# Two mixtures of experts: outputs stored and gathered, or scaled by GpSimd and added by indirect DMA into two sums

## What is computed

```python
expert_weight, expert_idx = jax.lax.top_k(probs, TOP_K)
expert_weight = expert_weight / jnp.sum(expert_weight, axis=-1, keepdims=True)
...
inter = jnp.square(jax.nn.relu(inter))
outb = jnp.einsum('ecf,edf->ecd', inter, w2_stack)
flat_out = outb[sorted_e, local_pos] * sorted_w[:, None]
moe_out = jnp.zeros((t, Cc), x.dtype).at[sorted_tok].add(flat_out)
```

## Time and profile before

| | |
|---|---|
| median of 3 runs | 1416.88 us (1414.7 to 1422.69) |
| the profiled execution | 1425.25 us |
| its span, first to last instruction | 1423.4 us |
| mean granted clock of TensorE | 0.878 of full |
| TensorE busy | 1079.6 us, 76% |
| VectorE busy | 748.6 us, 53% |
| ScalarE, GpSimd busy | 385.5 us and 357.9 us |
| moved by DMA | 113.59 MB |

### The profile page before, as it was taken

One profiled execution on the slowest core, in us unless ns is written; L12 is line 12 of the kernel. 1 busy time (PEld: TensorE's weight loads), 2 busy tenths in 40 slices (PEclk: granted clock), 3 DMA queues, 4 the chain that ended last, 5 costly groups with the idle time before them and its releaser, 6 DMA issues.

```text
span 1423.4 us, 16288 instructions
## 1 busy us (share of the span) xinstructions
PE 1079.6 (76%) x5482; PEld 882.7 (62%) x5482; DVE 748.6 (53%) x1778; ACT 385.5 (27%) x705; POOL 357.9 (25%) x290
## 2 busy tenths in 40 slices
PE   1987989788746673788999747989897159999940
PEld 0646766477545653566878535868685058999840
DVE  5467555565533436355556553454535536666642
ACT  1204022031123324224242232332422023333310
POOL 4204144040402234411010131010101432224235
PEclk9999989999878996799999957989999569999985
DMA  8700014000156652100000010000000664636435
GB/s 265 238 1 30 0 63 130 1 0 0 60 176 194 177 182 69 43 17 0 1 0 0 15 58 16 1 1 0 0 1 1 195 189 141 185 109 217 148 97 169
DMA packets 91887, 113.59 MB, mean 80 GB/s; under 512 B 6577, under 2 KB 77489, under 8 KB 91697
## 3 DMA queue, kind: packets, MB, share of 16 engines
q1 hardware_dynamic: 72480, 78.46, 16.9%
q0 software_dynamic: 19344, 34.35, 8.4%
HBM read 76.09 MB, written 36.70 MB: 79 GB/s over the span
## 4 chain that ended last, share of the span: by engine, by line
PE 46%; issue 17%; DVE 15%; POOL 5%; DMA 5%; ACT 5%; SPq 3%; another core or an unknown queue 0%; DVEq 0%; POOLq 0%; ACTq 0%
PE PS L194 11%; PE PS L196 10%; PE PS L195 10%; PE PS L1594 6%; DMA xg<-routed 3%; PE PS L1513 2%; POOL routed L773 2%; POOL HB L833 2%; PE PS L1488 1%; POOL rstd L766 1%; PE PS L1409 1%; DVE SM L1329 1%; PE PS L1577 1%; PE PS L1536 1%; DVE RT L1064 1%
## 5 line engine op out<-in xcount | busy, mean ns | idle before, releaser
L766 POOL TENSOR_TENSOR rstd<-ve,minus_half 128x4 f32<-128x4 f32 x40 | 40.6, 1015 | 412.0 <-DVE ve L1056 254.6
L194 PE MATMUL PS<-xt,split 128*128 128x256 f32 x412 | 121.9, 296 | 14.2 <-issue 11.1
L195 PE MATMUL PS<-xt,split 128*128 128x256 f32 x412 | 119.9, 291 | 0.0
L196 PE MATMUL PS<-xt,split 128*128 128x256 f32 x412 | 119.6, 290 | 0.0
L1594 PE MATMUL PS<-VP,HB 128*128 128x257 f32 x384 | 94.9, 410 | 15.6 <-DVE VP L1342 15.6
L452 POOL TENSOR_TENSOR split<-raw,split 128x1024 fp32r<-128x1024 f32 (+1 forms) x15 | 66.7, 4444 | 140.4 <-DMA raw<-down_w 86.5
L1594 PEld LDWEIGHTS PS<-VP,HB 128*128 128x128 f32 x384 | 78.8, 207 | 33.5 <-DVE VP L1342 20.6
L194 PEld LDWEIGHTS PS<-xt,split 128*128 128x128 f32 x412 | 82.8, 201 | 17.9 <-issue 14.0
L773 POOL DMA_INDIRECT routed<-S,dest x64 | 65.5, 1024 | 99.5 <-DVE dest L1127 82.3
L194 PE MATMUL PS<-split,hs 128*128 128x256 f32 x244 | 78.6, 322 | 11.6 <-DVE hs L512 10.1
L195 PEld LDWEIGHTS PS<-xt,split 128*128 128x128 f32 x412 | 82.7, 201 | 0.0
(11 more groups left out here) (299 smaller groups left out, 2768.6 us busy)
## 6 DMA issues: line engine op xcount, KB each, us to landing
xg<-routed SPq DMA_DIRECT2D x44, 256.0 KB, 2.8
outputs<-y SPq DMA_DIRECT2D x40, 256.0 KB, 3.4
outputs<-zeros SPq DMA_DIRECT2D x3, 2048.0 KB, 16.1
routed<-zeros SPq DMA_DIRECT2D x20, 256.0 KB, 4.6
raw<-m_w SPq DMA_DIRECT2D x16, 256.0 KB
split<-m_w POOLq DMA_DIRECT2D x16, 256.0 KB, 4.0
x_base<-X SPq DMA_DIRECT2D x8, 512.0 KB
raw<-gate_w SPq DMA_DIRECT2D x8, 512.0 KB, 7.7
```

The source lines that it names most:

```text
L194: pe.matmul(out_, a[1], b[0], start=first, stop=False)
L195: pe.matmul(out_, a[0], b[1], start=False, stop=False)
L196: return pe.matmul(out_, a[0], b[0], start=False, stop=last)
L766: pool.tensor_tensor(rstd[h][:], ve[h][:], minus_half[:], ALU.pow).then_inc(sem("rstd_ready"), 1)
```

## The change

Outputs are no longer stored and gathered. Each row of `routed` carries, behind its 256 channels, its token's number and its weights for the 8 experts (`W` = 265 columns, written by the router with the row); the filling blocks carry a row number beyond the tokens. ScalarE copies these columns of a group to `meta_next` (`keep`), GpSimd takes them to `meta` (`take_meta`). For each group GpSimd scales the two halves of `y` (128 rows each) into `scaled` and adds each with an indirect DMA that adds: the first half to `x_base`, which for the second mixture is the kernel's output `out`, the second half to a second sum, `x_add`. No two additions to one sum are in flight together. Behind layer 0 SP loads both sums, and VectorE adds them (`combine`, one step a batch). In the second mixture the two sums are merged by one adding DMA ahead of the last expert, whose halves then both go to `out`.

Weights are loaded only once, by SP, to two raw buffers, two experts ahead; ScalarE copies them to the high half ahead of an expert's groups, and VectorE (layer 0) or GpSimd (second mixture) makes the low half. Layer 0's first two experts keep the casting DMA. Two of the eight fills stand ahead of the first group now, six behind the second group's load; in layer 0 the attention's weights follow them. `moe_end` doesn't wait for the outputs' landing; SP and GpSimd do (`added_up`).

```diff
 
-        x_base = nc.dram_tensor("x_base", (2, B, T, D), F32, kind="Internal").ap()
-
-        routed = [nc.dram_tensor(f"routed{m}", (XROWS, D), F32, kind="Internal").ap() for m in range(2)]
-        outputs = nc.dram_tensor("outputs", (NG * G, D), F32, kind="Internal").ap()
+        x_base = [nc.dram_tensor("x_base", (B * T + P, D), F32, kind="Internal").ap(), out]
+
+        x_add = [nc.dram_tensor(f"x_add{m}", (B * T + P, D), F32, kind="Internal").ap() for m in range(2)]
+        sums = list(zip(x_base, x_add))
+        routed = [nc.dram_tensor(f"routed{m}", (XROWS, W), F32, kind="Internal").ap() for m in range(2)]
...
-        share = [sb(f"share{m}", [P, B, TT, 2]) for m in range(2)]
         carry = sb("carry", [P, TT + 1, E])
-        expert_of = sb("expert_of", [P, B, TT, 2])
-        source = sb("source", [P, B, TT, 2], I32)
...
             w.cols = C * f * w.ups + w.fc * D
-            w.raw = sb(f"raw{m}", [P, w.cols], F32, st)
+            w.raw = [sb(f"raw{m}", [P, w.cols], F32, st)[:], (S0[0][:].rearrange("p c t -> p (c t)") if m == 0 else
...
+                                ("kept", total + 1), ("down", total), ("y", total + 1)):
                 eng.wait_ge(sem(f"m{m}_{name}"), value)
 
                 eng.sem_inc(sem("passed"), 1)
 
+        def added_up(eng, m, total):
+
+            for name, value in ((("yout0", 16 * total + 16), ("yout1", 16 * total + 16)) if m == 0 else (("yout0", 32 * total + 16),)):
+                eng.wait_ge(sem(f"m{m}_{name}"), value)
+                eng.sem_inc(sem("passed"), 1)
+
...
-            w = moe[m]
-            if e:
-                sp.wait_ge(sem(f"m{m}_lo"), e)
+            i = raw_buffer(m, e)
+            used = [f for f in range(e) if raw_buffer(m, f) == i]
+            if used:
+                sp.wait_ge(sem(f"m{m}_lo"), used[-1] + 1)
             for ap, at, n in expert_sources(m, e):
-                sp.dma_start(w.raw[:, at:at + n].rearrange("p (c o) -> p c o", c=ap.shape[1]), ap).then_inc(sem(f"m{m}_raw"), 16)
+                sp.dma_start(moe[m].raw[i][:, at:at + n].rearrange("p (c o) -> p c o", c=ap.shape[1]), ap).then_inc(sem(f"m{m}_raw{i}"), 16)
...
-            for e in range(3):
-                fill(sp, m, e, "first_filled")
-            sp.wait_ge(sem("first_filled"), 48 * (m + 1))
-            sp.wait_ge(sem("filled"), 16 * (4 + m * (E - 3)))
-            sp.wait_ge(sem("outputs_filled"), 48)
+            for e in range(2):
+                fill(sp, m, e, "filled")
             for h in two:
                 sp.wait_ge(sem(f"scattered{h}"), 16 * 2 * TT * PAIRS * (m + 1))
+            sp.wait_ge(sem("filled"), 16 * (6 + 2 * (m + 1)))
             group_in(sp, m, 0)
-            for e in range(3, E):
-                fill(sp, m, e, "filled")
-
-        def moe_sp(sp, m, more):
-            w = moe[m]
+
+        def moe_sp(sp, m):
             sp.wait_ge(sem(f"m{m}_turned"), 1)
+            sp.wait_ge(sem(f"m{m}_kept"), 1)
             group_in(sp, m, 1)
+            for e in range(2, E):
+                fill(sp, m, e, "late_filled")
+            if m == 0:
+                attention_weights(sp)
+            sp.wait_ge(sem("late_filled"), 16 * (E - 2) * (m + 1))
             for e in range(E):
-                if e == 1:
-                    sp.wait_ge(sem("filled"), 16 * (4 + (m + 1) * (E - 3)))
-                if e == (2, 0)[m]:
-                    more(sp)
-                if 1 <= e < E - 1:
-                    raw_in(sp, m, e + 1)
+                if e + 2 < E:
+                    raw_in(sp, m, e + 2)
                 lo, hi = bounds(sp, m, e)
                 with sp.Fori(lo, hi) as t:
                     group_in(sp, m, t + 2)
-                    counted(sp, m)
-                    sp.wait_ge(sem(f"m{m}_y"), t + 2)
-                    sp.dma_start(outputs[bass.ds(t * G, G), :].rearrange("(a p) d -> p a d", p=P), w.y[:]).then_inc(sem(f"m{m}_yout"), 16)
             moe_end(sp, m, hi)
...
+        def weights_hi(act, m, e, done=None):
 
             w = moe[m]
-            if e >= 2:
-
-                done = pool.value_load(table[m][0:1, e - 1:e], min_val=1, max_val=NG - 1)
-                counted(pool, m)
-                pool.wait_ge(sem(f"m{m}_down"), done)
...
+                act.wait_ge(sem(f"m{m}_down"), done)
+                act.sem_inc(sem("passed"), 1)
+            act.wait_ge(sem(f"m{m}_raw{i}"), raw_loads(m, e))
+            act.activation(w.split[e % 2][:, 0], w.raw[i], ACT.Copy).then_inc(sem(f"m{m}_whi"), 1)
 
...
+            a_step = 16 * (1 + m)
+
+            def take_meta(n):
+
+                pool.wait_ge(sem(f"m{m}_kept"), n)
+                pool.sem_inc(sem("passed"), 1)
+                pool.tensor_copy(meta[:], meta_next[:]).then_inc(sem(f"m{m}_meta"), 1)
+
...
+            def add_rows(t, e):
+
+                for a in range(G // P):
+                    pool.wait_ge(sem(f"m{m}_meta"), t + 1)
+                    if m == 0 or e < E - 1:
+                        landed, value, total = sem(f"m{m}_yout{a}"), (16 + a_step * t if a == 0 else 16 + 16 * t), sums[m][a]
+                    else:
+                        landed, value, total = sem("m1_yout0"), 16 + 32 * t + 16 * a, sums[m][0]
+                    if m == 0 or e < E - 1 or a == 0:
+                        pool.wait_ge(landed, value)
+                    pool.wait_ge(sem(f"m{m}_y"), t + 2)
...
+                    pool.sem_inc(sem("passed"), 1)
+                    pool.indirect_dma_start(out=total, out_offset=bass.IndirectOffsetOnAxis(ap=to_row[:, a:a + 1], axis=0),
+                                            in_=scaled[:, a], in_offset=None, compute_op=ALU.add)\
+                        .then_inc(landed, a_step if a == 0 and e < E - 1 else 16)
+
+            for a in range(2):
+                pool.dma_start(sums[m][a][B * T:B * T + P], pad[:, 0:D]).then_inc(sem(f"m{m}_yout{a}"), 16)
+            if m == 0:
+                attention_weights_hi(pool)
             pool.wait_ge(sem(f"m{m}_table"), 1)
-            for e in range(2, E):
...
-                    attention_weights_hi(pool)
-                weights_hi(pool, m, e)
-                weights_lo(pool, m, e)
+            for h in two:
+                pool.wait_ge(sem(f"x_out{h}"), 16 * PAIRS * (m + 1))
+            take_meta(1)
+            for e in range(E):
+                if m == 1 and e < E - 1:
+                    if e == 0:
+                        pool.wait_ge(sem("m1_lo"), 1)
+                    weights_lo(pool, m, e + 1)
+                lo, hi = bounds(pool, m, e)
+                if m == 1 and e == E - 1:
+                    counted(pool, m)
+                    for name, value in (("yout0", 32 * lo + 16), ("yout1", 16 * lo + 16)):
+                        pool.wait_ge(sem(f"m1_{name}"), value)
+                        pool.sem_inc(sem("passed"), 1)
+                    pool.dma_start(out[0:B * T], x_add[1][0:B * T], accum_op=ALU.add, max_dma_last_dim=4096).then_inc(sem("merged"), 16)
+                    pool.wait_ge(sem("merged"), 16)
+                with pool.Fori(lo, hi) as t:
+                    counted(pool, m)
+                    add_rows(t, e)
+                    take_meta(t + 2)
+            moe_end(pool, m, hi)
+            added_up(pool, m, hi)
...
+            def keep(n):
+                act.wait_ge(sem(f"m{m}_xg"), 16 * n)
+                if not isinstance(n, int):
+                    act.wait_ge(sem(f"m{m}_meta"), n - 1)
+                act.activation(meta_next[:], w.xg[:, :, D:W], ACT.Copy).then_inc(sem(f"m{m}_kept"), 1)
...
             x_hi(1)
+            keep(1)
             for e in range(E):
                 lo, hi = bounds(act, m, e)
+                if 1 - m <= e < E - 1:
...
-                if m == 0 and n >= 2:
-                    dve.wait_ge(sem(f"second_in{h}"), 32)
+            def combine(n, h):
...
-                dve.wait_ge(sem(f"rows{h}"), 16 * 2 * TT * (m * PAIRS + n // 2 + 1))
-                for kk in range(2):
-                    for j in range(TT):
-                        ins = dve.scalar_tensor_tensor(out=x_t[:, j], in0=rows_h[h][:, kk, j], scalar=share[m][:, n, j, kk:kk + 1],
-                                                       in1=x_t[:, j], op0=ALU.mult, op1=ALU.add)
-                        if kk == 1 and j == TT - 1:
-                            ins.then_inc(sem("combined"), 1)
-                        elif j == TT - 1:
-                            step(ins)
-                            chained()
+                    dve.wait_ge(sem(f"second_in{h}"), 48)
+                x_t = residual(n, h)
+                dve.tensor_tensor(x_t[:], x_t[:], added[n], ALU.add).then_inc(sem("combined"), 1)
 
 
```

More of the change, by code:

```diff
@@ L496, in moe_act @@
                         h_hi(t, w.fc - 1)
+                    keep(t + 2)
             if m == 0:
@@ L1397, in _ @@
             moe_dve(dve, 1)
-            for pair in range(PAIRS):
-                for n, h in of_pair[pair]:
-                    combine(1, n, h)
         @block.tensor
```

221 lines of the change are left out of this document (108 added, 113 removed), and 4 rows, old and new, of the table ORDER_C.

## The result

The changed kernel takes 1434.8 us (median of 4 runs, 1434.15 to 1435.46), the kernel before 1415.8 beside it: ratio 1.0126, interval 1.009 to 1.0162. It is slower by 1.3%, where I had forecast 1384 and faster, and it lies 7 us above my range.

A forecast was written before the change was run, and what follows sets the result against it. TensorE bounds the second mixture, rows late behind SP's queue layer 0. Tail -26.4, layer 0 +1.6, attention's start -6.8, second mixture's start -4.5 and its loop +3 sum to -33 us: 1384, range 1358 to 1428.

The forecast's parts named there:

- GpSimd's work for one half of a group: Scaling 0.4 us, cast 0.27, wait 0.1, scatter 1.02 and 0.30: 2.1 a half, 5.0 a group with metadata and allowance.
- three competing cycles: Layer 0, per group: TensorE 4.9 us, GpSimd waiting for the last addition 5.2, the metadata loop 5.75; 5.9 taken.
- the loop: Layer 0: ScalarE's `keep` waits for GpSimd's metadata copy, SP's next fetch for `keep`: 5.75 us a group, 5.9 taken.
- My sign for the loop: In layer 0 TensorE would wait for rows, with ScalarE's `keep` behind GpSimd; output copies 5.9 us apart.
- L: Time from the end of an adding scatter's issue to its landing: 3.4 us taken, ends 1.5 and 7.1.
- M: Merge of 2.1 MB into `out` in the second mixture's tail: 18 us taken, ends 8 and 40.
- late landing: Rival: additions land late, 1426 us at L = 6; slower than the kernel before from L = 5.9; chance 0.19.
- The tail: From the seventh expert's last output to the end: 48 us instead of 74, a change of -26.4.
- The front of layer 0: First output at 409.2, a wait of about 9 us for the third group's rows, second output at 422.5.
- The weight loads: Layer 0: freed SP, two raw buffers, high halves on ScalarE, low on VectorE: 0.9 us a group, nearly all taken back.
- The attention and the second mixture's start: From layer 0's last output to the second mixture's first: -6.8 us at the attention's start, -4.5 ahead of the mixture.
- The base: The -33 us were taken off the median of 1416.88; the profiled execution took 1425.25, 8.4 above it.

The follow-up runs named there:

- run 4: Changed kernel with layer 0's metadata kept in a slot for each group: 1420.1 us, ratio 1.0017 to the kernel before, 7.54 us a group.
- run 11: Changed kernel with layer 0's metadata in slots and its scaling cut to 16 of 256 columns: 1394.3 us, ratio 0.9812, 6.43 us a group.
- run 9: Changed kernel with layer 0's outputs stored, gathered and combined as in the kernel before: 1377.6 us, ratio 0.9709, 4.85 us a group.
- run 3: Changed kernel with both halves scaled first in layer 0, one wait, then both adding scatters: 1453.4 us, ratio 1.0225, 8.81 us a group.
- run 8: Changed kernel with the second mixture adding everything into the output, one sum and no merge: 1453.4 us, ratio 1.0161.
- run 12: Kernel before with only the change's weight loads, outputs still stored and gathered: 1400.0 us, ratio 0.9873, 5.42 us a group.
- run 2: Changed kernel with layer 0's scatters writing instead of adding: 1413.0 us, ratio 0.9958, 7.20 us a group.
- run 5: Changed kernel with VectorE scaling and casting in layer 0, metadata in slots: 1418.6 us, ratio 0.9913, 7.10 us a group.

## Why the prediction was wrong

**GpSimd's work for one half of a group** is the step that failed: "That is 2.1; two halves and the copy of `meta` are 4.5", 5.0 with the allowance. Measured it is 3.5 a half (scaling 0.92 for 0.4, the idle time ahead of the scatter 0.8 for 0.1, scatter 1.62 for 1.02 and 0.30 behind it, cast 0.18 for 0.27) and 7.6 a group with the metadata. Among my three competing cycles GpSimd's whole work for a group was not even one. At 5.0 GpSimd lies below TensorE and the loop, and the 5.9 follows; at 7.6 it is the bound itself, with 0.3 of the loop on top. 17 x (7.88 - 5.9) = 34 us, two thirds of the whole error. Runs 4 and 11 show it by the periods of 7.6 and 6.4 that follow GpSimd's own sum. My sign for the loop, TensorE waiting for rows with `keep` behind GpSimd, came true all the same: it shows who is late, and not that the loop is the bound. My own rows had a warning: a line drawn between the two that I named gives 0.47 for a scaling, and by columns the 6.83 of the earlier trace rows gives 0.57; I took 0.4. The 0.8 and the addition's 0.6 stood in no row, and I gave this term no ends, as I did L and M.

TensorE's own part grew with its waits. From the first output to the last it is busy 72.8 us before, 86.8 after and 68.6 in run 9, at a granted clock of 0.90, 0.78 and 0.95, for the same work: of the 45 us that this stretch grew, 14 are a slower TensorE and 31 are waits. As GpSimd sets the period, the 14 are no cost of their own.

**L** was named as the first thing to go wrong and was right within its ends: 2.3 for 3.4. The late landing's 1426 is near the result for another reason; landings enter only where nothing covers them (run 3) or where all halves share a sum (run 8). (By my own sum L stands five times in the tail, and not four as the rivals had it.) The Trainium skill ("DMA: Bandwidth & Descriptors", anatomy of one DMA) gives 2.0 us and the bytes for a DMA of GpSimd's; here an addition takes 3.9 from its issue's start, and the page of the profile has 2.6 for the plain scatters. It does make a difference, and 0.6 of it is GpSimd's own issue.

**M** was 14.4 for 18, again inside. Two million bytes of zeros into a sum land in 14.9 us in the same kernel, so this addition from HBM to HBM took no longer than such a fill. Whether an inline add runs at half a copy's rate (the Trainium skill, "Collectives: The Full Stack", why ReduceScatter is half of AllGather) can't be seen here; no run has the plain copy to set beside it.

**The tail** took 53.2 instead of 48: 1.7 more ahead of the merge and 6.6 more behind it, both by the scaling and the 0.8 above, 3.1 less in the merge:

```profile
1385.52 1.62 POOL L515 DMA_INDIRECT x_add<-S,to_row  x1 [0.79 <-POOL to_row L510]
...
1390.00 1.18 POOL L538 DMA_DIRECT2D out<-x_add  x1 [2.63 <-DMA x_add<-S,to_row]
1404.94 0.92 POOL L509 TENSOR_SCALAR S<-y,meta 128x256 f32<-128x256 f32 x1 [13.76 <-DMA out<-x_add]
...
1407.67 1.70 POOL L515 DMA_INDIRECT out<-S,to_row  x1 [1.67 <-issue]
...
1412.28 1.62 POOL L515 DMA_INDIRECT out<-S,to_row  x1 [1.80 <-DMA out<-S,to_row]
```

**The front of layer 0** was right in mechanism: a wait of 13.67 for the third group's rows ("about 9"), second output at 424.21 (422.5). That the second output fits has luck in it, since the first came at 405.43 (409.2 said), and between the traces named above it moves by 10 us. **The weight loads** were right too: "worth 0.9 us a group; the new loop takes nearly all of it back". Run 9 gives 1.2. It was taken back by GpSimd's work.

**The attention and the second mixture's start** came out at -11.4 for -11.3, but not by my parts. The attention began 6.9 us after the last output (3.2 before), and by the code's order TensorE waits there for the last `kept` and for the rows fetched behind it:

```profile
565.04 3.48 PE L1588 MATMUL PS<-HB 128*128 128x256 f32 x8 [7.00 <-issue]
```

The additions took 1.22 each as said, and the shorter combinations did save 4.3 us: from the attention's first matmul to the router's first product it is 276.34 us (565.04 to 841.38), and 280.64 in run 12, which gathers and combines as before (511.38 to 792.02). The later start takes 3.7 of it back, where I had counted 2.5 won, so this stretch is 636.0 here and 636.9 and 636.3 in runs 9 and 12. TensorE's wait ahead of the second mixture is 17.5 for 21.8 as forecast, in run 12 too, so that is the weight loads' part. And half of the -11.4 is none of the change's. In the profiled execution of the kernel before VectorE stands still twice:

```profile
603.92 0.16 DVE L1348 TENSOR_SCALAR SM<-PS 128x4 f32<-128x4 f32 x1 [6.97 <-remote]
...
609.59 0.69 DVE L1329 TENSOR_REDUCE SM<-PS 128x1 f32<-128x512 f32 x1 [3.60 <-remote]
```

"Remote" is a releaser that the profile doesn't know, and the waits of no other run here show one. Against run 12 this place costs 5.6 us. What was behind it stays open. Without it the stretch is some -6 for -11.3: that the two numbers agree is luck.

**The base** made 8 us: I took the profiled execution's distance from its median (8.4) off the forecast, and the changed kernel's profiled one has none (1434.15). The 5.6 us above may be part of that distance; then 5.5 of these 8 us are the attention's miss. With one trace of the kernel before this isn't shown.

## What to carry to other kernels

Before work is moved to an engine that was idle, its instructions are to be priced one by one at their dearest nearby row, the idle time ahead of a DMA's issue among them, and set against the period of the loop it joins: 7.6 us of work a group joined a loop of 6. Scatters that add pay where the time behind them is the program's end (21 us here), not inside a loop that is shorter than GpSimd's work for them (7.6 us a group beside TensorE's 4.9). And a bundle is best taken apart before it is judged: of this one, weight loads and layer 2's additions were worth 41 us, and one part cost 57.

## What the runs showed of the hardware

An adding indirect DMA of 128 rows of 1 KB keeps GpSimd for 1.62 us (plain 1.04, run 2) and lands 3.9 after its issue began; in run 8 the next one on the same sum mostly starts 4.6 to 4.7 after the last. GpSimd's scaling of 128x256 by a column takes 0.92 us (of 128x16 0.33, run 11), VectorE's 0.35. About 0.8 us pass between the end of the instruction that a scatter waits for and the scatter, whether GpSimd or VectorE made the result (runs 4 and 5), and 0.30 between two scatters without such a wait (run 3). A copy of 128x18 is shown at 0.22 behind a plain scatter and 0.78 behind an adding one. TensorE's granted clock in layer 0 was 0.90 with the engine busy 68% of the time, 0.78 with 57% and 0.95 with 69%, and its work took 72.8, 86.8 and 68.6 us.
